# A layer norm over features, moved from all-ones matmuls to transposes and VectorE statistics, with the stages of each loop step in another order

## What is computed

```python
for i in range(6):
    x = attn_layer(shift_tokens(x), Wqkv[i], q_scale[i], k_scale[i], Wo[i]) + x
    x = ffn_layer(shift_tokens(x), ln_g[i], ln_b[i], W1[i], b1[i], W2[i], b2[i]) + x

def ffn_layer(x, g, bln, W1, b1, W2, b2):
    mu = x.mean(-1, keepdims=True)
    var = ((x - mu) ** 2).mean(-1, keepdims=True)
    xn = (x - mu) / jnp.sqrt(var + 1e-05) * g + bln
    hg = xn @ W1 + b1                      # 128 -> 2 x 341
    a, gate = jnp.split(hg, 2, -1)
    return a * gelu(gate) @ W2 + b2
```

## Time and profile before

| | |
|---|---|
| three runs, median | 3431.78 us (3429.99 to 3432.28) |
| profiled execution, its own time | 3432.49 us |
| its span, first to last instruction | 3430.7 us |
| PE busy | 3290.3 us, 96% |
| PEld | 2578.9 us, 75% |
| DVE | 2628.7 us, 77% |
| ACT | 2683.1 us, 78% |
| POOL | 2361.1 us, 69% |

### The profile page before, as it was taken

The page is one execution under the profiler, slowest core; times in us unless marked ns, Lnnn a source line. Parts: engine busy times, 40 slices in busy tenths (PEclk is TensorE's granted clock), DMA queues, the critical chain, the costliest instruction groups (busy, mean ns, idle before and its releaser), DMA issues. The chain is left out here.

```text
span 3430.7 us, 124638 instructions
## 1 busy us (share of the span) xinstructions
PE 3290.3 (96%) x50165; PEld 2578.9 (75%) x50165; DVE 2628.7 (77%) x5823; ACT 2683.1 (78%) x5501; POOL 2361.1 (69%) x1568
## 2 busy tenths in 40 slices
PE   7979999999999999999999999999999999999997
PEld 5758777777777777777777777777777777777774
DVE  4558878878878877887877887877788777788783
ACT  3438888888888887888888888888888888888884
POOL 2028767777777776776777777777677677777771
PEclk9989999999999999999999999999999999999998
DMA  2001111211111211111211211121111121111111
GB/s 85 2 6 50 44 37 46 68 39 50 42 41 45 69 41 39 53 44 36 71 42 38 53 43 40 43 67 44 44 46 43 39 71 39 47 44 45 41 40 46
DMA packets 98187, 156.44 MB, mean 46 GB/s; under 512 B 18128, under 2 KB 39632, under 8 KB 96720
## 3 DMA queue, kind: packets, MB, share of 16 engines
q1 hardware_dynamic: 93440, 132.73, 14.3%
q10 hardware_dynamic: 4176, 15.74, 1.4%
HBM read 20.48 MB, written 2.10 MB: 7 GB/s over the span
## 5 line engine op out<-in xcount | busy, mean ns | idle before, releaser
L314 POOL TENSOR_TENSOR qks<-work 128x1024 f32<-128x1024 f32 x384 | 910.0, 2370 | 72.0 <-issue 62.8
L322 POOL TENSOR_TENSOR qkr<-qks,rnorm 128x1024 f32<-128x1024 f32 x384 | 731.4, 1905 | 321.0 <-issue 296.9
L330 POOL TENSOR_TENSOR probn<-prob,psumr 128x512 f32<-128x512 f32 x384 | 400.6, 1043 | 390.5 <-DVE psumr L1109 390.5
L498 ACT ACTIVATE sq<-psum 128x512 f32<-128x512 f32 x768 | 464.9, 605 | 184.1 <-PE psum L747 180.6
L747 PE MATMUL psum<-whi,xhi 128*128 128x512 f32 x1152 | 563.5, 489 | 20.5 <-POOL xlo L339 14.6
L1085 DVE TENSOR_TENSOR work<-psum,rot 128x512 f32<-128x512 f32 x768 | 508.1, 662 | 63.9 <-POOL qks L314 52.1
L1061 DVE TENSOR_REDUCE ssq<-sq 128x8 f32<-128x512 f32 x768 | 514.1, 679 | 42.6 <-ACT sq L498 16.0
L767 PEld LDWEIGHTS psum<-kT,qbd 128*64 128x64 f32 x12288 | 393.6, 139 | 172.2 <-issue 136.7
L747 PE MATMUL psum<-whi,xlo 128*128 128x512 f32 x1152 | 459.7, 399 | 0.0
L767 PE MATMUL psum<-kT,qbd 128*64 128x64 f32 x12288 | 447.0, 226 | 12.4 <-ACT kT L534 12.4
L747 PE MATMUL psum<-wlo,xhi 128*128 128x512 f32 x1152 | 455.9, 396 | 0.0
(11 more groups left out here) (132 smaller groups left out, 6496.2 us busy)
## 6 DMA issues: line engine op xcount, KB each, us to landing
vsh<-vtok SPq DMA_DIRECT2D x384, 192.0 KB, 2.4
vsh<-vtok SPq DMA_DIRECT2D x384, 64.0 KB, 2.9
xsh<-xs_in SPq DMA_DIRECT2D x192, 64.0 KB, 2.4
ff_x<-x_mid SPq DMA_DIRECT2D x96, 128.0 KB, 2.4
wqkv<-Wqkv_dram ACTq DMA_DIRECT2D x5, 1536.0 KB, 7.6
wo_next<-Wo_dram ACTq DMA_DIRECT2D x5, 512.0 KB, 9.6
xtok<-x_dram SPq DMA_DIRECT2D x4, 512.0 KB, 10.9
out_dram<-qkr SPq DMA_DIRECT2D x8, 256.0 KB, 2.6
```

The costliest lines, as they stand in the source:

```text
L314: pool.tensor_tensor(qks[:, :, :], rcos, rsin, ALU.add).then_inc(s["add_ready"], 1)
L322: pool.tensor_tensor(qkr[:, n % 2, :, :], qks[:, :, :], rnorm[:, :].unsqueeze(2).to_broadcast([P, 2 * OCT, DH]), ALU.mult).then_inc(s["qkr ...
L330: pool.tensor_tensor(probn[:, :, :], prob[:, n % 2, :, :], psumr[:, n % 2, 1, :].unsqueeze(2).to_broadcast([P, OCT, KEYS]), ALU.mult).then ...
L498: act.activation(sq[:, w * OCT:(w + 1) * OCT, :], bank[w].rearrange("p (h n) -> p h n", n=DH), ACT.Square).then_inc(s[("sqq_ready", "sqk_r ...
```

## The change

The mean and the variance are no longer made by PE. PE transposes the block's four 128x128 pieces (`ffn_tokens`, at place 1 between `turn_k` and `attend`), so that tokens lie on partitions; DVE takes statistics of each (`bn_stats`, `bn_aggr`) and applies them (`tensor_scalar` with the mean and 1/sqrt of each token), both at place 2; ACT's Ln and Exp now work on 128x4 values, at place 2, between the two; PE transposes back (`ffn_features`, at the end of place 2), and ACT applies g and b while it empties bank 4, at place 3. POOL has no part of it any more, nor is there a Square. The constant matrix goes.

`ffn_up` stands at the end of place 3 instead of the head of place 4 and waits for `aot_ready` only before its second gate. `ffn_down` stands at place 4, after `attend`, instead of at place 5. The fetch is at place 1. On all four engines the order of the other stages of every step is changed too.

```diff
@@ pool loop
-                ffn_normed(block_at(step, 4))
+                rotary_gains(step)
                 x_low(step)
-                rotary_gains(step)
@@ act
             def ffn_inverse(b):
-                act.wait_ge(s["f_v"], b + 1)
-                act.activation(ff_n[:, :], bank[4], ACT.Ln, bias=eps_row[:, 0:1]).then_inc(s["f_ln"], 1)
+                act.wait_ge(s["f_mv"], b + 1)
+                act.activation(fvar[:, :], fmv[:, :, 1], ACT.Ln, bias=eps_row[:, 0:1]).then_inc(s["f_ln"], 1)
                 act.wait_ge(s["f_ln"], b + 1)
-                act.activation(ff_n[:, :], ff_n[:, :], ACT.Exp, scale=-0.5).then_inc(s["f_rs"], 1)
+                need(act, "f_no", b)
+                act.activation(frstd[:, :], fvar[:, :], ACT.Exp, scale=-0.5).then_inc(s["f_rs"], 1)
@@ act loop
-                ffn_square(block_at(step, 2))
                 mask_seeded(step - 3)
+                ffn_inverse(block_at(step, 2))
                 x_high(step)
                 k_turned(step - 3)
-                exponential(step - 4)
-                ffn_affine(block_at(step, 4))
-                ffn_inverse(block_at(step, 3))
                 attended(step - 6)
                 ffn_gates(block_at(step, 4))
+                ffn_affine(block_at(step, 3))
+                exponential(step - 4)
...
                 probabilities_turned(step - 5)
+                square(step, 1)
                 values(step - 3)
-                square(step, 1)
@@ pe
+            def ffn_tokens(b):
+                pe.wait_ge(s["f_x"], b * 32 + 32)
+                need(pe, "f_out", b)
+                need(pe, "pts_ready", min(b * UNROLL + 2 * UNROLL + 1 - 4, STEPS))
+                for i in range(TPI):
+                    mm = pe.transpose(bank[4][:, i * P:(i + 1) * P], ff_x[:, i * P:(i + 1) * P], ident[:, :])
+                mm.then_inc(s["f_t1"], 1)
...
             def ffn_up(b):
...
-                need(pe, "f_u", b * CH)
-                need(pe, "pts_ready", min(step - 5, STEPS))
-                need(pe, "aot_ready", min(step - 5, STEPS))
+                need(pe, "pts_ready", min(step - 4, STEPS))
                 for ch in range(CH):
                     w = CW[ch]
+                    if ch == 1:
+                        need(pe, "f_u", b * CH)
+                        need(pe, "aot_ready", min(step - 4, STEPS))
@@ pe loop
-                ffn_up(block_at(step, 4))
                 projection(step, 0)
-                ffn_down(block_at(step, 5))
                 scores(step - 3)
                 turn_q(step - 2)
...
+                projection(step, 1)
                 value_projection(step - 3)
-                projection(step, 1)
                 turn_k(step - 2)
+                ffn_tokens(block_at(step, 1))
                 attend(step - 5, block_at(step, 4))
+                ffn_features(block_at(step, 2))
+                ffn_down(block_at(step, 4))
                 output(step - 6)
-                ffn_mean(block_at(step, 0))
-                ffn_variance(block_at(step, 2))
+                ffn_up(block_at(step, 3))
@@ dve
+            def ffn_statistics(b):
+                dve.wait_ge(s["f_t1"], b + 1)
+                for i in range(TPI):
+                    dve.bn_stats(fst6[:, i, :], bank[4][:, i * P:(i + 1) * P]).then_inc(s["f_st"], 1)
+                for i in range(TPI):
+                    dve.wait_ge(s["f_st"], b * TPI + i + 1)
+                    ins = dve.bn_aggr(fmv[:, i, :], fst6[:, i, :])
+                ins.then_inc(s["f_mv"], 1)
+            def ffn_normed(b):
+                dve.wait_ge(s["f_rs"], b + 1)
+                for i in range(TPI):
+                    ins = dve.tensor_scalar(ff_x[:, i * P:(i + 1) * P], bank[4][:, i * P:(i + 1) * P], fmv[:, i, 0:1],
+                                            frstd[:, i:i + 1], ALU.subtract, ALU.mult)
+                ins.then_inc(s["f_no"], 1)
@@ dve loop
                 inverse_sum(step - 5)
+                ffn_statistics(block_at(step, 2))
                 rotation(step - 1, 1)
-                ffn_centred(block_at(step, 1))
+                ffn_normed(block_at(step, 2))
+                square_sum(step - 1, 1)
                 ffn_out(block_at(step, 5))
                 residual(step - 7)
+                guarded(step - 1)
                 probability_sum(step - 4)
-                guarded(step - 1)
                 ffn_gated(block_at(step, 4))
                 row_maximum(step - 3)
+                square_sum(step, 0)
                 below_maximum(step - 3)
                 rotation(step, 0)
-                square_sum(step, 0)
-                square_sum(step, 1)
```

More of the change, by code:

```diff
@@ L239, in _ @@
                 x_half(step)
-                ffn_fetched(block_at(step, 0))
+                ffn_fetched(block_at(step, 1))
                 values_shifted(step - 4)
@@ L571, in ffn_affine @@
                 layer = b // BLOCKS
-                act.wait_ge(s["f_xn"], b + 1)
-                act.activation(ff_n[:, :], ff_x[:, :], ACT.Identity, scale=lng_col[:, layer:layer + 1],
+                act.wait_ge(s["f_t2"], b + 1)
+                need(act, "f_a", b * CH)
+                act.activation(ff_n[:, :], bank[4], ACT.Identity, scale=lng_col[:, layer:layer + 1],
                                bias=lnb_col[:, layer:layer + 1]).then_inc(s["f_xnT"], 1)
@@ L861, in ffn_up @@
                     return
-                step = (b + 2) * UNROLL + 4
+                step = (b + 2) * UNROLL + 3
                 layer = b // BLOCKS
```

46 lines of the change are left out of this document (20 added, 26 removed).

## The result

| | runs | median, us | lowest to highest |
|---|---|---|---|
| before | 4 | 3431.63 | 3429.99 to 3432.28 |
| after | 4 | 3338.24 | 3335.76 to 3341.10 |

The ratio is 0.9731, with a 95% interval of 0.9719 to 0.9743. The kernel is 93 us faster; 84 had been forecast. The profiled execution of after has a span of 3339.3 us.

What follows compares the result with a forecast made beforehand. The prediction took PE, packed but for one hole per block, as the bound. Hole 52 + mean and variance against transposes 33 - boundaries 4 + drain 3 = 84 us off 3431.8 gave 3347, with an 8-in-10 range of 3332 to 3390.

Steps and rivals of the forecast that it cites:

- PE bounds the steps: PE's stream is packed except for one hole per block, so what is saved on PE comes back in full.
- The hole, 52 us: Places 3 to 4: PE's lost time before the gates, mostly waiting for `aoT`, closes; 1.11 us a block, 52 us.
- The rival with the thin cover: Place 4's Exp or the v copy comes some tenths late at a few steps; half the hole lost, 3373, 9%.
- Mean and variance against transposes, 33 us: On PE, mean and variance matmuls (1.70 us a block) give way to eight transposes (1.00); 0.70 a block, 33 us.
- the lower end of the bounds: Eight transposes hold PE for 0.87 us, from the spacing of eight in a row; 1.00 was taken, 1.20 the upper end.
- DVE, nothing: DVE's new work at place 2, 2.25 us with 3.0 allowed, is covered at both deadlines, so it costs nothing.
- the moved sum of squares: On DVE, k's sum of squares moves behind the place 2 work, so DVE gets there half of 1.49 us earlier.
- Boundaries, 4 us lost: At five layer boundaries `rotary_gains` ahead of `x_low` on POOL adds 0.73 us to PE's wait; 4 us lost.
- The drain, 3 us: At the kernel's end, the chain from the last mean's matmul to the last gates shrinks from 8.3 to 5.3; gain 3.
- Gelu straight behind the load: On ACT at place 4, no 1380 ns drain at table switches; with it the gain would fall by 42 us.

Runs made afterwards that it cites:

- e1: The changed kernel with each of the two groups of four transposes per block issued twice; 3376.62 us, 0.9842 of before.
- e9: The changed kernel with the wait for `aoT` ahead of the first gate again and the softmax's Exp ahead of `aoT` again; 3348.96 us, 0.9764 of before.
- e6: The kernel before with one edit on ACT, the softmax's Exp behind the Gelus; 3450.98 us, 1.0055 of before.
- e7: The kernel before with PE waiting for `aoT` only from the second gate on and the Exp behind the Gelus; 3428.23 us, 0.9992 of before.
- e12: The kernel before with the gates' wait split, the Exp behind the Gelus and `guarded` ahead of `probability_sum` on DVE; 3402.37 us, 0.9915.
- e2: The changed kernel with four more statistics per block on DVE at place 2, 0.75 us more; 3349.74 us, 0.9763 of before.
- e3: The changed kernel with twelve more statistics per block on DVE at place 2, 2.25 us more; 3430.85 us, 0.9999 of before.
- e4: The changed kernel with DVE's old order: `guarded` behind the sum of the exponentials, both sums of squares at the step's end; 3381.14 us, 0.9858 of before.
- e10: The changed kernel with `x_low` ahead of `rotary_gains` on POOL, as before the change; 3329.04 us, 0.9707 of before.

## Why the prediction was right, and where it wasn't

The forecast was 3347 us, the time is 3338. By its steps:

- **PE bounds the steps.** Right. e1's added transposes came out in full, and the wins are the matmuls' own durations (0.85 at place 0).
- **The hole, 52 us.** Right: 13.95 to 12.84. But its reasoning that ACT's order alone closes it holds only for the changed kernel as a whole. e9 shows that the Exp's move gives 0.2 and the rest 0.9, and e6, e7 and e12 that the Exp's move has a price of its own (in e6 alone it loses 65.33 - 64.86 = 0.47 a block net), which `guarded` ahead of the sum on DVE takes away in part. The rival with the thin cover was about this, at the wrong place: it looked for the Exp's delay at `ffn_gated` and the turn of the probabilities at place 4; it comes out at `guarded` and the k transposes of place 3.
- **Mean and variance against transposes, 33 us.** Mis-sized. Eight transposes cost 0.86 (e1) and not 1.00. The net is 0.84 a block, 39 us, and the lower end of the bounds, which was worked out from the spacing of eight in a row, was the right one.
- **DVE, nothing.** Right for the sum, wrong in its reason. The work was 2.3 to 2.5 us, as thought. The cover is 0.5 (e2, e3), not 1.2 or 2.3, since the first deadlines are neither the bank of the probabilities nor that of q. They are what ACT has queued, in order, behind two small operations that wait for DVE: 0.48 at its Ln over 128x16, 0.97 at its Ln over 128x4. One more pass of 0.7 at place 2 and the change would have paid for it.
- **The order of DVE's other stages.** Worth 43 us (e4), and no term of the sum. The prediction counted the moved sum of squares as 0.7 us of extra cover and held that the norm was covered without it; it did not look at `guarded`. This is the step that is missing. The forecast held because the new order is part of the change. By its own reasoning, the same change without the new order would have been put at 3347 too, as e4's expectation did, and that time is 3381, inside the range but by luck.
- **Boundaries, 4 us lost.** 2.7 seen, the wait from 1.94 to 2.62. By the medians the better order (e10) is 9 us faster; 3.4 of that is the wait, and the rest, in which the clock's falls have a part, is open.
- **The drain, 3 us.** 2.3 to 2.8, right.
- **Gelu straight behind the load.** On the way out too: the Exp starts where the second load ends, with nothing between them.

```profile
1510.92 1.28 ACT L576 ACT_TABLE_LOAD   x1
1512.21 0.63 ACT L547 ACTIVATE prob<-sdiff 128x512 f32<-128x512 f32 x1
```

The load takes 1.28 us, and 1510.92 + 1.28 = 1512.20. Ahead of it there is no gap either: the last Gelu starts at 1510.22 and takes 0.68. The Trainium skill ("ScalarE: Activation LUTs", What ACT_TABLE_LOAD costs) has the same 1283 ns for the load and adds some 1380 ns of drain to each switch; this trace shows no such drain on either side of the load, and the measurement decides.

By the spans the gain is 91.4 and not 84. 47 x (1.92 - 1.81) = 5 us of the difference are the blocks (mostly the transposes), 1 the boundaries, 1 the first scores that come earlier, which no step had. That one is scatter: they start between 241.5 and 245.7 in the fourteen traces, whatever the edit. The medians differ by 2 more than the two profiled executions, which is their scatter. Open is why the clock falls behind one wait and not behind an equal one, how e4's 0.83 divides between its two parts, and what the new norm would bring in the kernel before with nothing else changed, which no run has.

## What to carry to other kernels

A cover isn't the distance to the buffer that is wanted next: follow every in-order engine that waits for the late one, and ask what it has queued behind that wait. Here the binding deadlines all went through ACT, at a 128x4 or a 128x16 operation of 0.2 to 0.3 us behind which stood the copies that PE needs. In this loop an operation of 0.2 us that feeds another engine did better ahead of a wide one that waits for something: that one exchange was worth 26 us between e7 and e12, and it is part of the order on DVE that was worth 43 us of 93. Edits which fill each other's gaps are best tried together and taken out one by one.

## What the runs showed of the hardware

- A group of four 128x128 transposes in float32 is recorded with 0.60 us and costs a packed PE 0.42 to 0.44, 0.11 each (e1).
- With twelve such transposes in each step and eight more in each block the granted clock is 1.00 over the 600 us from 900 to 1500 (after).
- Statistics over four tiles of 128x128 in PSUM are recorded with 0.84 us, the four aggregations with 0.36, four `tensor_scalar` with 1.36. From SBUF the statistics took 0.86; half of eight aggregations and half of eight `tensor_scalar` are 0.32 and 1.07. With PSUM as the source the last is dearer and the statistics are not.
- Behind waits of 1.92 to 1.95 us at a layer's start the granted clock fell at 20 of 30 boundaries, behind waits of 2.60 to 2.64 at 23 of 35: the scores took up to 1.98 us instead of 1.15, and a fall cost about 1.5 us. Between these two lengths of the wait no difference is seen in how often it happens.
